# Probability-times-values matmuls issued for two key steps at a time, from one ring of four probability slots

## The chip, the cores and the metric

The kernel runs on one core of a Trainium2 chip. The metric is the device time of one execution in microseconds (us). Five engines matter: TensorE (PE, matmuls, with its weight loads shown apart as PEld), VectorE (DVE), ScalarE (ACT), GpSimd (POOL), and the DMA queue of SyncE (SP).

## What is computed

One transformer layer: a layer norm, then a latent attention and a mixture of experts side by side, both added to the input. The change lies in the attention (2 batches, 1024 tokens, 16 heads), whose core in the reference is:

```python
q_latent = x @ wq_down                       # 192 wide
kv_latent = x @ wkv_down                     # 64 wide
...
q_r = apply_rope(q_r, cos, sin)
k_r = apply_rope(k_r, cos, sin)
q = jnp.concatenate([q_c, q_r], axis=-1)
k = jnp.concatenate([k_c, k_r], axis=-1)
scores = jnp.einsum('bthd,bshd->bhts', q, k) * scale
scores = jnp.where(causal[None, None], scores, jnp.finfo(scores.dtype).min)
probs = jax.nn.softmax(scores, axis=-1)
out = jnp.einsum('bhts,bshd->bthd', probs, v).reshape(b, t, H * D)
return out @ wo
```

The kernel multiplies the probabilities with the 64 wide latent instead of `v`; `wv_up` and `wo` are folded into one matrix per head.

## The kernel before

The program has three parts: `prepare` (layer norm, latents), `attend` (attention, from about 50 to 875 us of the profile) and `mix` (the experts). Only `attend` is changed.

**Stages and steps.** `attend` runs 16 stages, s = 0 to 15: 8 pairs of heads times 2 batches (b = 0 and 1). A stage has 12 steps k. Steps 0 to 3 handle query chunk c = 0 (512 queries) against key tiles j = 0 to 3 (128 keys each), steps 4 to 11 chunk c = 1 against key tiles j = 0 to 7. Steps 0 to 3 and 8 to 11 are diagonal: their widths are 512, 384, 256 and 128 queries. In each step e = 0 and e = 1 are the two heads. Tensors are held transposed, keys on the partitions, queries along the free axis.

**What one step does.** PE computes `scores` (k, e) into one of three PSUM banks `ps_s` (lines 592 to 601). ACT takes the exponential into a probability buffer in SBUF (`exponent`, line 734). PE multiplies it with the latent: `values` (line 613) adds into the bank `ps_o`, head 0 in rows 0 to 63 and head 1 in rows 64 to 127, so that its matmuls are 64 columns wide in the array, where scores, projections and pieces are 128 wide. The text calls the pair of matmuls of step k v(k). Being float32, each of the two shows as two passes in the trace, four records in all. DVE (head 0) and POOL (head 1) add the probabilities up for the softmax's denominator (`add_probs`, lines 908 and 1060).

**Where probabilities stand.** Those of j = 0 go to `first`, one buffer per chunk and head, which is also the running sum. Those of all other steps go round a ring of three slots.

**The denominator.** PE sums the running sum over the keys with a matrix of ones (`row_sums`, line 634, also 64 wide): `Lp` for chunk 1 of the stage before, in step 2, and `L0` for chunk 0, in step 4. DVE then takes the reciprocal `rec` (line 913) and the product `on` (line 917), ACT and POOL split `on` into `ohi` and `olo` (lines 782, 1064), and PE projects them out (`Yp0`, `Yp1`, `Y0`, `Y1`, lines 644 to 646).

**Work for the next stage.** In steps 0 to 3 PE projects queries and keys of the next stage (`QR0`, `KR0`, `QR1`, `KR1`, `QL0`, `QL1`, line 550), which DVE, POOL and ACT rotate and split. From step 5 to step 11 PE computes 24 pieces p0 to p23 of the next stage's raw scores (line 566, line 569 on the diagonal), from which DVE takes row maxima (line 897). All these side products share two banks `ps_x`, and the pieces share two banks `ps_m`: p(n) waits for the maximum of p(n-2), and each side product for the reader of the one two places before.

**Order.** Every engine runs its own list in order. PE's is written by hand in `body`: `scores(k, 0)`, piece slot 0, side work 0, `scores(k, 1)`, slot 1, `values(k - 1)`, slot 2, side work 1, slot 3. The tables are

```python
PIECE_AT = dict(zip([(5, 3)] + [(k, n) for k in (6, 7, 8, 9, 10) for n in range(4)] + [(11, n) for n in range(3)],
SIDE = {(0, 0): ["QR0"], (0, 1): ["KR0"], (1, 0): ["QR1"], (1, 1): ["KR1"], (2, 0): ["Lp"], (2, 1): ["QL0"], (3, 1): ["QL1"],
        (4, 1): ["L0"], (6, 0): ["Yp0"], (6, 1): ["Yp1"], (7, 0): ["B"], (7, 1): ["WA"], (10, 0): ["Y0"], (10, 1): ["Y1"]}
```

so p0 is in step 5, p1 to p4 in step 6, p5 to p8 in step 7, p9 to p12 in step 8, p13 to p16 in step 9, p17 to p20 in step 10 and p21 to p23 in step 11. `B` and `WA` are weight folds of stages with b = 0 only. The last stage has no pieces and no projections.

Of the kernel before, what the change touches and what calls it, by code (L numbers as in the profile page):

```python
# [21 lines left out]
F32 = mybir.dt.float32  # L22
# [330 lines left out]
RING = 3  # L353


def ring_of(k):

    r = k - 1 if k < TPC else k - 2
    steps = [s for s in range(STEPS) if s not in (0, TPC)]
    if r >= RING:  # L360
        return r % RING, steps[r - RING]
    last = max(q for q in range(len(steps)) if q % RING == r % RING)
    return r % RING, steps[last] - STEPS
# [18 lines left out]
SIDE = {(0, 0): ["QR0"], (0, 1): ["KR0"], (1, 0): ["QR1"], (1, 1): ["KR1"], (2, 0): ["Lp"], (2, 1): ["QL0"], (3, 1): ["QL1"],  # L382
# [16 lines left out]
def attend(nc, d, keep):  # L399
    ctx = ExitStack()  # L400
    with ctx:
# [11 lines left out]
        t1, first, ring, shift, oe, rec, on, ohi, olo = tensors(nc, ctx, [  # L413
            ("t1", [P, 4, CH], F32), ("first", [P, 2, 2, CH], F32), ("ring", [P, RING, 2, CH], F32),
# [34 lines left out]
        def probs(k, e):  # L449
            c, j, off, _ = step_of(k)  # L450
            if j == 0:
                return first[:, c, e, off:]
            return ring[:, ring_of(k)[0], e, off:]

        def sums(s, c, j, e):


            return (sum_pool if e else sum_dve), s * 10 + (3 + j if c else j)
# [48 lines left out]
        def _(pe):  # L507
# [119 lines left out]
            def row_sums(i, b, name, s, c):  # L627

                for e in range(2):
                    pe.wait_ge(*sums(s, c, 7 if c else 3, e))  # L630

                def products(out):
                    for e in range(2):
                        mm = nc.tensor.matmul(out[64 * e:64 * e + 64, :], ones[:, 0:64], first[:, c, e, :], start=True, stop=True)  # L634
                    return mm
                side(i, b, name, products)
# [12 lines left out]
            def body(i):  # L649
                for b in range(B):  # L650
# [3 lines left out]
                    for k in range(STEPS):  # L654
# [45 lines left out]
            s = 2 * PAIRS - 1  # L700
            values(s, 1, STEPS - 1, alone=True)
# [5 lines left out]
            for e in range(2):  # L707
                mm = nc.tensor.matmul(ps_x[n % 2][64 * e:64 * e + 64, :], ones[:, 0:64], first[:, 1, e, :], start=True, stop=True)
# [9 lines left out]
        def _(act):  # L718
            def exponent(s, k, e):
# [3 lines left out]
                if j:  # L723

                    _, before = ring_of(k)
                    ge(act, pv_done, s * U + 2 * before + e + 1)
                    if before >= 0:
                        cb, jb, _, _ = step_of(before)
                        sb = s
                    else:  # L730
                        cb, jb, _, _ = step_of(before + STEPS)
                        sb = s - 1
                    ge(act, *sums(sb, cb, jb, e))
                nc.scalar.activation(probs(k, e), ps_s[(2 * k + e) % 3][:, off:], ACT.Exp, scale=SCALE).then_inc(exp_done, 1)  # L734

            def first_free(i, b, c):

                if c == 0:
                    if b == 1:
                        act.wait_ge(misc_ready, misc(i, 0, "L0")[0] + 1)  # L740
                    elif not is_first(i):
                        act.wait_ge(misc_ready, misc(i, 0, "QR0")[0] - 2)
                elif b == 1 or not is_first(i):
                    act.wait_ge(misc_ready, misc(i, b, "Lp")[0] + 1)
# [98 lines left out]
        def _(dve):  # L843
# [55 lines left out]
            def add_probs(s, k):  # L899
# [38 lines left out]
            def body(i):  # L938
                for b in range(B):
                    s = i * 2 + b  # L940
                    earlier = b == 1 or not is_first(i)
                    for k in range(STEPS):
# [25 lines left out]
                        if k % TPC or k > TPC:  # L968
                            add_probs(s, k)
# [53 lines left out]
        def _(pool):  # L1023
# [27 lines left out]
            def add_probs(s, k):  # L1051
# [3 lines left out]
                if j == 1:  # L1055

                    pool.wait_ge(pv_done, s * U + 2 * (k - 1) + 2)
                else:
                    pool.wait_ge(*sums(s, c, j - 1, 1))
                nc.gpsimd.tensor_tensor(first[:, c, 1, off:], first[:, c, 1, off:], probs(k, 1), ALU.add).then_inc(sum_pool, 1)  # L1060
# [5 lines left out]
            def body(i):  # L1066
                for b in range(B):
# [5 lines left out]
                    for k in range(1, TPC):  # L1073
                        add_probs(s, k)
# [4 lines left out]
                    for k in range(TPC + 1, STEPS):  # L1079
                        add_probs(s, k)  # L1080
# [350 lines left out]
```

## Time and profile before

| quantity | value |
| --- | --- |
| median of 3 runs | 1288.75 us (1288.48 to 1288.90) |
| profiled execution, span of the trace | 1286.1 us |
| PE busy | 1223.4 us (95%) |
| DVE busy | 905.4 us (70%) |
| POOL busy | 674.5 us (52%) |
| ACT busy | 589.7 us (46%) |

The span is the time from the first to the last instruction of one profiled execution; it is 2.65 us under the median of the runs. Matmuls overlap in the array and their ends are modelled, so the time that a matmul costs is read from its start to the start of the next one, not from its duration. A time in square brackets behind a row of a timeline is how long the engine sat idle before it, and whom it waited for.

### The profile page before, as it was taken

How to read it: one execution, taken by the hardware profiler on the slowest of the kernel's cores; microseconds unless marked ns; L12 is line 12 of the kernel's file. 1: busy time of each engine (PE TensorE's matmuls, PEld its weight loads, DVE VectorE, ACT ScalarE, POOL GpSimd, SP SyncE). 2: the span in 40 equal slices, each digit the busy share in tenths (PEclk: the TensorE clock that was granted, in tenths of full speed). 3: DMA queues.
4: the chain of work that ended last, by engine and by line, in shares of the span. 5: the costliest groups of instructions: out<-in, count | busy, mean ns of one | idle time of the engine just before them, and what ended most of it. 6: DMA issues, size and time to landing. Idle time of an engine off the chain costs nothing. (4 is left out here: it accounts for less than half of the span.)

```text
span 1286.1 us, 20218 instructions
## 1 busy us (share of the span) xinstructions
PE 1223.4 (95%) x5904; PEld 806.2 (63%) x5952; DVE 905.4 (70%) x1410; ACT 589.7 (46%) x1192; POOL 674.5 (52%) x546
## 2 busy tenths in 40 slices
PE   5898899999999999999999999998999999999997
PEld 3555455555555555555555555546788887888886
DVE  6679878879888888888888798764544445444444
ACT  3453535545545445455355365453433333333332
POOL 1176766677677667676676676652233332323332
PEclk9999999999999999999999999998999999999999
DMA  5001001001000000000100001015633333433332
GB/s 200 33 1 33 1 1 33 1 1 32 0 0 15 16 0 13 18 0 0 32 0 0 15 0 58 1 26 147 180 114 114 114 114 100 134 114 114 114 114 90
DMA packets 26442, 67.33 MB, mean 52 GB/s; under 512 B 3044, under 2 KB 9700, under 8 KB 26408
## 3 DMA queue, kind: packets, MB, share of 16 engines
q1 hardware_dynamic: 26264, 66.84, 17.2%
q8 instruction: 17, 0.28, 0.1%
q14 instruction: 17, 0.14, 0.0%
q10 hardware_dynamic: 144, 0.07, 0.0%
HBM read 62.42 MB, written 4.47 MB: 52 GB/s over the span
## 5 line engine op out<-in xcount | busy, mean ns | idle before, releaser
L734 ACT ACTIVATE ring<-ps_s 128x512 f32<-128x512 f32 (+3 forms) x320 | 146.5, 468 | 309.3 <-PE ps_s L601 308.4
L1333 POOL TENSOR_TENSOR hl<-hf,hh 128x512 fp32r<-128x512 f32 x96 | 123.4, 1286 | 288.9 <-ACT hh L1270 288.9
L897 DVE TENSOR_REDUCE nm<-ps_m 128x1 f32<-128x512 f32 (+3 forms) x370 | 196.4, 549 | 46.0 <-PE ps_m L569 39.1
L1060 POOL TENSOR_TENSOR first<-first,ring 128x512 f32<-128x512 f32 (+3 forms) x160 | 161.2, 1007 | 89.6 <-ACT ring L734 57.1
L908 DVE TENSOR_TENSOR first<-first,ring 128x512 f32<-128x512 f32 (+3 forms) x160 | 140.6, 879 | 10.1 <-ACT ring L734 5.1
L1029 POOL TENSOR_TENSOR xtf<-xtf,sinv 128x512 f32<-128x512 f32 x62 | 79.6, 1284 | 119.1 <-DVE xtf L851 119.1
L1302 DVE TENSOR_TENSOR gs<-gs,routing 128x512 f32<-128x512 f32 x64 | 44.3, 692 | 137.8 <-ACT gs L1266 137.8
L613 PE MATMUL ps_o<-ring,kvn 128*64 128x512 f32 (+3 forms) x640 | 132.4, 493 | 0.0
L1270 ACT ACTIVATE hh<-hf 128x512 fp32r<-128x512 f32 x96 | 60.7, 633 | 121.1 <-DVE hf L1307 121.1
L1266 ACT ACTIVATE gs<-ps_g 128x512 f32<-128x512 f32 x96 | 57.4, 598 | 121.3 <-PE ps_g L1225 121.3
L913 DVE RECIPROCAL rec<-ps_x 128x512 f32<-128x512 f32 x32 | 107.3, 3352 | 4.8 <-PE ps_x L634 4.0
L596 PE MATMUL ps_s<-shift,ones 128*128 128x512 bf16 (+3 forms) x336 | 109.7, 327 | 0.0
L1047 POOL TENSOR_TENSOR qlo<-t,qhi 64x512 fp32r<-64x512 f32 x64 | 94.9, 1483 | 8.6 <-POOL first L1060 2.6
L596 PEld LDWEIGHTS ps_s<-shift,ones 128*128 128x128 bf16 x384 | 37.2, 97 | 89.9 <-issue 52.0
L599 PE MATMUL ps_s<-qhi,khi 128*128 128x512 f32 (+1 forms) x192 | 87.6, 456 | 0.0
L599 PE MATMUL ps_s<-qhi,keys 128*128 128x512 f32 (+1 forms) x192 | 87.2, 454 | 0.0
L850 DVE TENSOR_TENSOR t<-ps_x,cosv 128x512 f32<-128x512 f32 x64 | 44.2, 691 | 58.6 <-PE ps_x L550 58.4
L1064 POOL TENSOR_TENSOR olo<-on,ohi 128x512 fp32r<-128x512 f32 x31 | 42.3, 1365 | 81.4 <-ACT ohi L782 81.4
L1031 POOL TENSOR_TENSOR t<-t,xtf 128x512 f32<-128x512 f32 x62 | 82.3, 1327 | 4.9
L566 PE MATMUL ps_m<-khi,qhi 128*128 128x512 f32 (+1 forms) x192 | 73.1, 390 | 8.8 <-DVE nm L897 8.6
L566 PE MATMUL ps_m<-keys,qhi 128*128 128x512 f32 (+3 forms) x178 | 68.1, 400 | 5.6 <-DVE nm L897 5.6
L1307 DVE TENSOR_TENSOR hf<-gs,ps_u 128x512 f32<-128x512 f32 x96 | 66.1, 688 | 9.9 <-PE ps_u L1225 0.6
(241 smaller groups left out, 3097.1 us busy)
## 6 DMA issues: line engine op xcount, KB each, us to landing
routing<-wT_scratch SPq DMA_DIRECT2D x34, 256.0 KB, 3.7
raw_a<-in_e SPq DMA_DIRECT2D x17, 384.0 KB, 3.0
cosv<-in_e SPq DMA_DIRECT2D x17, 384.0 KB, 3.0
sinv<-wT_scratch SPq DMA_DIRECT2D x17, 384.0 KB, 3.6
raw<-in_e SPq DMA_DIRECT2D x17, 384.0 KB, 3.0
routing<-wT_scratch SPq DMA_DIRECT2D x16, 384.0 KB, 3.3
raw_a<-in_a SPq DMA_DIRECT2D x8, 512.0 KB, 3.3
raw_b<-in_b SPq DMA_DIRECT2D x8, 480.0 KB, 3.9
```

The source lines that it names most:

```text
L566: mm = nc.tensor.matmul(out[:, 0:keys], qhi[b][e][:, t * P:(t + 1) * P], khi[b][e][:, k0:k0 + keys], start=True, stop=not diagonal)
L596: nc.tensor.matmul(out[:, off:], ones16[:, :], shift[:, c, e, off:], start=True, stop=False)
L599: nc.tensor.matmul(out[:, off:], khi[b][e][:, kk], qhi[b][e][:, q], start=False, stop=False)
L613: nc.tensor.matmul(ps_o[64 * e:64 * e + 64, off:], kvn[:, b * 8 + j, :], probs(k, e), start=j == 0, stop=last).then_inc(pv_done, 1)
L734: nc.scalar.activation(probs(k, e), ps_s[(2 * k + e) % 3][:, off:], ACT.Exp, scale=SCALE).then_inc(exp_done, 1)
L897: nc.vector.tensor_reduce(out=to, in_=bank[:, 0:keys], axis=AXX, op=ALU.max, negate=True).then_inc(piece_max, 1)
L908: nc.vector.tensor_tensor(first[:, c, 0, off:], first[:, c, 0, off:], probs(k, 0), ALU.add).then_inc(sum_dve, 1)
L913: nc.vector.reciprocal(rec[:, :], ps_x[x][:, :]).then_inc(rec_done, 1)
L1031: nc.gpsimd.tensor_tensor(t1[:, g, :], t1[:, g, :], sh[:, g, :], ALU.add).then_inc(rope_sum, 1)
L1047: nc.gpsimd.tensor_tensor(lo[to_b][e][rows, cs], t1[rows, g, :], hi[to_b][e][rows, cs].bitcast(F32), ALU.subtract).then_inc(rope_lo, 1)
L1060: nc.gpsimd.tensor_tensor(first[:, c, 1, off:], first[:, c, 1, off:], probs(k, 1), ALU.add).then_inc(sum_pool, 1)
L1333: nc.gpsimd.tensor_tensor(hl[:, c, :], hf[:, c, :], hh[:, c, :].bitcast(F32), ALU.subtract).then_inc(h_lo, 1)
```

## The change

- `values` runs in even steps only, for two key steps at once: v(k-2) and v(k-1) in step k, and v(10) and v(11) of the stage before in step 0.
- The ring has four slots and takes all steps; `ring_of` and `first` are gone. A separate `total_p` holds the running sum: step j = 1 writes it from two ring slots, later steps add one slot. In chunk 0 the slot of j = 1 is only 384 wide, so the first 128 columns are copied apart, one more instruction on DVE and on POOL per stage.
- ACT's waits before an exponential name the slot's readers of four steps before. The wait for the row sums' buffer moves from ACT to DVE and POOL (`total_free`).
- `Lp` moves from step 2's first side slot to its second, right behind the values.

```diff
-RING = 3
-
-
-def ring_of(k):
...
+RING = 4
+assert STEPS % RING == 0
...
-SIDE = {(0, 0): ["QR0"], (0, 1): ["KR0"], (1, 0): ["QR1"], (1, 1): ["KR1"], (2, 0): ["Lp"], (2, 1): ["QL0"], (3, 1): ["QL1"],
+SIDE = {(0, 0): ["QR0"], (0, 1): ["KR0"], (1, 0): ["QR1"], (1, 1): ["KR1"], (2, 1): ["Lp", "QL0"], (3, 1): ["QL1"],
...
         def probs(k, e):
-            c, j, off, _ = step_of(k)
-            if j == 0:
-                return first[:, c, e, off:]
-            return ring[:, ring_of(k)[0], e, off:]
+            return ring[:, k % RING, e, step_of(k)[2]:]
...
-                    if e or alone:
+                    if alone or (e and k % 2):
                         pe.wait_ge(exp_done, s * U + 2 * k + e + 1)
...
-                        if k:
+                        if k and k % 2 == 0:
+                            values(s, b, k - 2)
                             values(s, b, k - 1)
-                        elif earlier:
+                        elif k == 0 and earlier:
+                            values(s - 1, 1 - b, STEPS - 2)
                             values(s - 1, 1 - b, STEPS - 1)
...
+                held = (k - RING) % STEPS
+                sb = s if k >= RING else s - 1
+                cb, jb, _, _ = step_of(held)
+                ge(act, pv_done, sb * U + 2 * held + e + 1)
+                ge(act, *sums(sb, cb, max(jb, 1), e))
                 nc.scalar.activation(probs(k, e), ps_s[(2 * k + e) % 3][:, off:], ACT.Exp, scale=SCALE).then_inc(exp_done, 1)
...
-            def add_probs(s, k):
+            def add_probs(i, b, s, k):
 
                 c, j, off, _ = step_of(k)
                 dve.wait_ge(exp_done, s * U + 2 * k + 1)
-                if j == 1:
-
-                    dve.wait_ge(pv_done, s * U + 2 * (k - 1) + 1)
+                if j > 1:
+                    dve.wait_ge(*sums(s, c, j - 1, 0))
                 else:
-                    dve.wait_ge(*sums(s, c, j - 1, 0))
-                nc.vector.tensor_tensor(first[:, c, 0, off:], first[:, c, 0, off:], probs(k, 0), ALU.add).then_inc(sum_dve, 1)
+                    total_free(dve, i, b, c)
+                so_far = total_p[:, c, 0, off:] if j > 1 else probs(k - 1, 0)[:, off:]
+                nc.vector.tensor_tensor(total_p[:, c, 0, off:], so_far, probs(k, 0), ALU.add).then_inc(sum_dve, 1)
+                if k == 1:
+                    nc.vector.tensor_copy(total_p[:, 0, 0, 0:P], probs(0, 0)[:, 0:P]).then_inc(sum_dve, 1)
```

POOL's `add_probs` is changed in the same way.

PE's list from the second piece of step 8 to the last piece of step 9. `ps_m` rows are pieces, `ps_o` rows are values. Before, p14 is followed by v(8), then p15 and p16:

```order
L566 MATMUL ps_m<-keys,qhi 128x512
L613 MATMUL ps_o<-ring,kvn 64x512 x2
L51 REGISTER_ALU
L566 MATMUL ps_m<-keys,qhi 128x256
L569 MATMUL ps_m<-ident,mask 128x128
L51 REGISTER_ALU
L566 MATMUL ps_m<-keys,qhi 128x512
```

Now p14, p15 and p16 stand in a row:

```order
L564 MATMUL ps_m<-khi,qhi 128x512
L51 REGISTER_ALU
L564 MATMUL ps_m<-khi,qhi 128x256
L567 MATMUL ps_m<-ident,mask 128x128
L51 REGISTER_ALU
L564 MATMUL ps_m<-khi,qhi 128x512
```

The values have left step 9; v(8) now stands in step 10 ahead of v(9), between p18 and p19.

PE's list in step 2, from the end of `scores(2, 0)` to the start of `QL0`. Before, `Lp` (line 634) stands between the scores of the two heads and v(1) behind them:

```order
L601 MATMUL ps_s<-qhi,keys 128x256
L634 MATMUL ps_x<-first,ones 64x512 x2
L596 MATMUL ps_s<-shift,ones 128x256
L598 MATMUL ps_s<-mask,ident 128x128
L599 MATMUL ps_s<-qhi,keys 128x256
L600 MATMUL ps_s<-qlo,keys 128x256
L601 MATMUL ps_s<-qhi,keys 128x256
L613 MATMUL ps_o<-ring,kvn 64x384 x2
L550 MATMUL ps_x<-q1hi,lhi 128x512
```

Now both scores come first, then v(0), v(1) and `Lp` in a row:

```order
L599 MATMUL ps_s<-qhi,khi 128x256
L51 REGISTER_ALU
L611 MATMUL ps_o<-ring,kvn 64x512 x2
L611 MATMUL ps_o<-ring,kvn 64x384 x2
L628 REGISTER_ALU
L511 REGISTER_ALU
L632 MATMUL ps_x<-total_p,ones 64x512 x2
L511 REGISTER_ALU
L548 MATMUL ps_x<-q1hi,lhi 128x512
```

`Lp` has moved behind `scores(2, 1)`, v(0) and v(1).

## Rows read from the trace of the kernel before

**Rows 1.** Steps 2-4, then 5-11: length, busy us of PE, PEld, DVE, ACT, POOL.

```profile
439.70:452.90 13.20, 12.65 (x66) 7.03 (x66) 12.86 (x13) 9.03 (x21) 8.05 (x8) 1.00 0.00 0
452.90:479.60 26.70, 26.25 (x136) 15.23 (x138) 23.00 (x36) 12.67 (x28) 21.61 (x17) 1.00 0.00 0
```

**Rows 2.** Timeline of PE around v(4) and v(0): start, us, operation, [idle before].

```profile
452.36 0.40 PE L600 MATMUL ps_s<-qlo,khi 128*128 128x512 f32 x1
452.60 0.39 PE L601 MATMUL ps_s<-qhi,klo 128*128 128x512 f32 x1
452.92 1.08 PE L613 MATMUL ps_o<-first,kvn 128*64 128x512 f32 x4
453.93 0.33 PE L566 MATMUL ps_m<-keys,qhi 128*128 128x128 f32 x1
...
439.09 0.50 PE L550 MATMUL ps_x<-kv,rhi 128*128 128x512 f32 x1
439.42 0.40 PE L550 MATMUL ps_x<-kv,rlo 128*128 128x512 f32 x1
```

**Rows 3.** Timeline of PE: v(11) alone; v(3) followed by L0, last stage.

```profile
434.27 0.44 PE L613 MATMUL ps_o<-ring,kvn 128*64 128x128 f32 x4
434.64 0.50 PE L550 MATMUL ps_x<-kv,rhi 128*128 128x512 f32 x1
...
840.48 0.44 PE L613 MATMUL ps_o<-ring,kvn 128*64 128x128 f32 x4
840.75 1.05 PE L634 MATMUL ps_x<-first,ones 128*64 128x512 f32 x4
```

**Rows 4.** Timeline of PE, steps 2 to 4: Lp, scores(2, 1), v(1), QL0, QL1, L0.

```profile
440.34 1.08 PE L634 MATMUL ps_x<-first,ones 128*64 128x512 f32 x4
441.35 0.28 PE L596 MATMUL ps_s<-shift,ones 128*128 128x256 bf16 x1
...
442.03 0.87 PE L613 MATMUL ps_o<-ring,kvn 128*64 128x384 f32 x4
442.83 0.50 PE L550 MATMUL ps_x<-q1hi,lhi 128*128 128x512 f32 x1
...
445.93 0.50 PE L550 MATMUL ps_x<-q1hi,lhi 128*128 128x512 f32 x1 [0.17 <-DVE rec L913]
...
449.96 1.08 PE L634 MATMUL ps_x<-first,ones 128*64 128x512 f32 x4 [0.39 <-DVE first L908]
```

**Rows 5.** Timeline of DVE, steps 2 to 5 of the same stage.

```profile
441.11 1.50 DVE L908 TENSOR_TENSOR first<-first,ring 128x384 f32<-128x384 f32 x1
442.53 3.35 DVE L913 RECIPROCAL rec<-ps_x 128x512 f32<-128x512 f32 x1
...
449.54 0.29 DVE L908 TENSOR_TENSOR first<-first,ring 128x128 f32<-128x128 f32 x1
...
454.95 1.66 DVE L917 TENSOR_TENSOR on<-oe,rec 128x512 f32<-128x512 f32 x1 [0.29 <-POOL olo L1064]
```

**Rows 6.** Timelines of POOL and PE, steps 5 and 6: olo, Yp0, v(5), p3.

```profile
453.54 1.27 POOL L1064 TENSOR_TENSOR olo<-on,ohi 128x512 fp32r<-128x512 f32 x1 [5.64 <-ACT ohi L782]
...
455.24 0.47 PE L644 MATMUL ps_x<-ohi,bhi 128*128 128x512 f32 x1
...
457.31 1.08 PE L613 MATMUL ps_o<-ring,kvn 128*64 128x512 f32 x4
458.70 0.49 PE L566 MATMUL ps_m<-keys,qhi 128*128 128x512 f32 x1 [0.32 <-DVE nm L897]
```

**Rows 7.** Timeline of DVE: p10, p11 and p12, add(8) in step 8; p19 in step 10.

```profile
466.66 0.69 DVE L897 TENSOR_REDUCE nm<-ps_m 128x1 f32<-128x512 f32 x1 [0.36 <-PE ps_m L566]
467.99 0.97 DVE L897 TENSOR_REDUCE nm<-ps_m 128x1 f32<-128x128 f32 x2 [0.65 <-PE ps_m L569]
468.88 1.65 DVE L908 TENSOR_TENSOR first<-first,ring 128x512 f32<-128x512 f32 x1
...
475.70 0.56 DVE L897 TENSOR_REDUCE nm<-ps_m 128x1 f32<-128x384 f32 x1 [0.54 <-PE ps_m L569]
```

More of the change, by code:

```diff
@@ L350, in step_of @@
     return c, j, max(0, j * P - c * CH), j * P >= c * CH
-RING = 3
-def ring_of(k):
[L358 to L363, printed above, removed]
+RING = 4
+assert STEPS % RING == 0
 def pieces():
@@ L412, in attend @@
         sh = keep["xtf"][:, :, :].rearrange("p k (g c) -> p (k g) c", c=CH)
-        t1, first, ring, shift, oe, rec, on, ohi, olo = tensors(nc, ctx, [
-            ("t1", [P, 4, CH], F32), ("first", [P, 2, 2, CH], F32), ("ring", [P, RING, 2, CH], F32),
+        t1, total_p, ring, shift, oe, rec, on, ohi, olo = tensors(nc, ctx, [
+            ("t1", [P, 4, CH], F32), ("total_p", [P, 2, 2, CH], F32), ("ring", [P, RING, 2, CH], F32),
             ("shift", [P, 2, 2, CH], BF16), ("oe", [P, CH], F32), ("rec", [P, CH], F32), ("on", [P, CH], F32),
@@ L449, in probs, with total_free @@
         def probs(k, e):
-            c, j, off, _ = step_of(k)
-            if j == 0:
-                return first[:, c, e, off:]
-            return ring[:, ring_of(k)[0], e, off:]
+            return ring[:, k % RING, e, step_of(k)[2]:]
         def sums(s, c, j, e):
-            return (sum_pool if e else sum_dve), s * 10 + (3 + j if c else j)
+            return (sum_pool if e else sum_dve), s * 11 + (4 + j if c else 1 + j)
+        def total_free(engine, i, b, c):
+            if c == 0:
+                if b == 1:
+                    engine.wait_ge(misc_ready, misc(i, 0, "L0")[0] + 1)
+                elif not is_first(i):
+                    engine.wait_ge(misc_ready, misc(i, 0, "QR0")[0] - 2)
+            elif b == 1 or not is_first(i):
+                engine.wait_ge(misc_ready, misc(i, b, "Lp")[0] + 1)
         def consumed(i, b, name):
@@ L633, in products @@
                     for e in range(2):
-                        mm = nc.tensor.matmul(out[64 * e:64 * e + 64, :], ones[:, 0:64], first[:, c, e, :], start=True, stop=True)
+                        mm = nc.tensor.matmul(out[64 * e:64 * e + 64, :], ones[:, 0:64], total_p[:, c, e, :], start=True, stop=True)
                     return mm
@@ L700, in _ @@
             s = 2 * PAIRS - 1
+            values(s, 1, STEPS - 2, alone=True)
             values(s, 1, STEPS - 1, alone=True)
@@ L707, in _ @@
             for e in range(2):
-                mm = nc.tensor.matmul(ps_x[n % 2][64 * e:64 * e + 64, :], ones[:, 0:64], first[:, 1, e, :], start=True, stop=True)
+                mm = nc.tensor.matmul(ps_x[n % 2][64 * e:64 * e + 64, :], ones[:, 0:64], total_p[:, 1, e, :], start=True, stop=True)
             mm.then_inc(misc_ready, 1)
@@ L722, in exponent @@
                 act.wait_ge(scores_ready, u + 1)
[L723 to L733, printed above, removed]
-                nc.scalar.activation(probs(k, e), ps_s[(2 * k + e) % 3][:, off:], ACT.Exp, scale=SCALE).then_inc(exp_done, 1)
[L736 to L744, printed above, removed]
+                held = (k - RING) % STEPS
[3 more added lines that the diff above has]
+                ge(act, *sums(sb, cb, max(jb, 1), e))
+                nc.scalar.activation(probs(k, e), ps_s[(2 * k + e) % 3][:, off:], ACT.Exp, scale=SCALE).then_inc(exp_done, 1)
             def latent_hi(i, b, c, to_b):
@@ L1049, in rope_low, with add_probs @@
                 pool.wait_ge(rope_lo, s * 8 + 2 * g + 2)
-            def add_probs(s, k):
+            def add_probs(i, b, s, k):
                 c, j, off, _ = step_of(k)
                 pool.wait_ge(exp_done, s * U + 2 * k + 2)
-                if j == 1:
-                    pool.wait_ge(pv_done, s * U + 2 * (k - 1) + 2)
-                else:
-                    pool.wait_ge(*sums(s, c, j - 1, 1))
-                nc.gpsimd.tensor_tensor(first[:, c, 1, off:], first[:, c, 1, off:], probs(k, 1), ALU.add).then_inc(sum_pool, 1)
+                if j > 1:
+                    pool.wait_ge(*sums(s, c, j - 1, 1))
+                else:
+                    total_free(pool, i, b, c)
+                so_far = total_p[:, c, 1, off:] if j > 1 else probs(k - 1, 1)[:, off:]
+                nc.gpsimd.tensor_tensor(total_p[:, c, 1, off:], so_far, probs(k, 1), ALU.add).then_inc(sum_pool, 1)
+                if k == 1:
+                    nc.gpsimd.tensor_copy(total_p[:, 0, 1, 0:P], probs(0, 1)[:, 0:P]).then_inc(sum_pool, 1)
             def out_low(s, c):
@@ L1079, in body @@
                     for k in range(TPC + 1, STEPS):
-                        add_probs(s, k)
+                        add_probs(i, b, s, k)
                         if k == 7:
```

6 lines of the change are left out of this document (2 added, 4 removed).

## The prediction, made before the result was known

> **What bounds the kernel now.** I read the page's busy shares first: PE 95%, DVE 70%. That suggests a kernel bound by PE, and the change takes work from PE. But DVE's 70% is an average over a part that hardly uses it (the experts) and the attention, so the second view is the busy time by stretch of one attention stage [rows 1]. In steps 2 to 4 DVE is busy 12.86 of 13.20 us; in steps 5 to 11 it is busy 23.00 of 26.70 us, while PE is busy 12.65 and 26.25. Both engines are nearly full, each in the other's cover. The third view, the timelines, shows where each waits for the other. PE waits for DVE at QL1 (0.17 us, for the reciprocal of Lp) and at L0 (0.39 us, for the last sum of chunk 0) [rows 4], and at p3 (0.32 us, for a maximum) [rows 6]. DVE waits for PE's pieces: 0.36 us for p10, 0.65 us for p11, 0.54 us for p19 [rows 7]. With two banks for pieces, neither can be more than two pieces from the other.
>
> **What one merge saves on PE.** An ordinary 512-column matmul follows its predecessor after 0.24 us (452.36 to 452.60), the first values matmul after 0.32 us, and the matmul behind a group also takes longer, 0.33 us (439.09 to 439.42) [rows 2]. So entering costs 0.08 and the successor 0.09 to 0.10 us. What a group itself loses is seen where two groups of this kind already follow each other: in the last stage L0 starts 0.27 us after v(3), while v(11), of the same 128 columns, holds PE for 0.37 us when it stands alone (434.27 to 434.64) [rows 3]. That is 0.10 us for leaving. A further 0.05 us is the first pass of a second group that needs no filling (L0 spans 1.05 us there, 1.08 elsewhere; I take the upper figure). The sum is about 0.33 us for a merge. Width: v(4) alone takes 1.01 us for 512 columns [rows 2], v(11) 0.37 us for 128 [rows 3], so 128 columns are 0.21 us and the bodies are 0.86, 0.64, 0.43 and 0.21 us for 512, 384, 256 and 128 columns.
>
> A stage has twelve values groups before and six after, so six merges, and Lp, which stood alone, joins v(1). Its successor is a bf16 matmul that pays nothing (the row of scores(2, 1) begins at once [rows 4]), so that merge gives 0.23 us. PE's work falls by 6 x 0.33 + 0.23 = 2.2 us per stage, 35 us over 16 stages.
>
> **What moves.** v(10) goes from step 11 into step 0 of the next stage, and the values of steps 1, 3, 5, 7 and 9 go one step later. So even steps get two values at once, up to 1.85 us in which PE makes no piece, and odd steps get none. I walk one stage from its first score and write how much later (+) or earlier (-) each point comes.
>
> *Steps 0 to 2.* v(10) comes in with its body less what is kept: +0.43 in step 0. v(0) leaves step 1: 0.86 body and 0.33 switch, -1.2. So PE arrives at step 2 0.8 us early. But Lp is now behind scores(2, 1) (0.68 us, 441.35 to 442.03 [rows 4]), v(0) and v(1). Its start is 440.34 - 0.8 - 0.08 + 0.68 + 0.05 + 0.86 + 0.64 = 441.7, its end 1.05 us later, 442.75. The reciprocal started at 442.53, held back only by DVE's own add(1), which began at 441.11 [rows 5]. It now waits for PE: **+0.2 us**. The new 128-column copy on DVE lies in this wait. The trace has no such copy; the nearest row is the 128-column sum with 0.29 us [rows 5], below is nothing. POOL's copy ends long before POOL's 5.64 us of idling ahead of olo [rows 6], so it costs nothing; if that cover were gone its price would be a POOL instruction, under the 1.27 us of a 512-column one.
>
> *Steps 2 to 4.* From the reciprocal on, DVE's chain sets the pace: reciprocal 3.35 us, on, sums and low parts without a gap, until add(3) ends at 449.83 and L0 starts at 449.96 [rows 4, 5]. QL1 needs the reciprocal's end, now 442.75 + 3.35 = 446.1 instead of 445.9. PE gets there much earlier than before: QL0 starts at about 442.65, and v(2) is no longer in between, so it arrives at about 444.8 and idles 1.3 us (0.17 before). L0 is bound by add(3) as before. So all that PE has saved by here, and the outgoing v(4) too, is idle time, and scores(5, 0) starts at **+0.2 us**.
>
> *Steps 5 to 7.* v(4) is gone from step 5 (-1.2), but Yp0 needs olo, which POOL ends at 454.81 [rows 6] and which hangs on the same chain: now 455.0, where PE would arrive at 454.25. And p2 needs the bank of p0, whose maximum follows on (454.95 to 456.61, moved by 0.2). So v(4) and v(5) start at +0.15 and last 0.86 us longer; the 0.32 us wait at p3 [rows 6] and the bound of p2 absorb some, p3 comes at +0.6. Step 7 has no values and gives 1.2 back, of which DVE, with four maxima and a sum in that step, lets through about half: scores(8, 0) at 0.
>
> *Steps 8 to 11.* v(6) and v(7) delay p11 and p12 by 0.84 us. DVE, which finished p10 at 467.35 and waited 0.65 us, now waits 1.5 us. Then come p11 to p16 with no values between them: DVE needs 0.97 us for p11 and p12 and up to 1.65 us for add(8) [rows 7], and two banks let PE no further ahead, so PE idles at p15 and p16 and gets to step 10 between 0.1 us (add(8) taking half its time) and 0.8 us late. v(8) and v(9) add 0.86 us ahead of p19: DVE waits about 1.4 us there instead of 0.54. Step 11 has lost v(10), but there DVE is the slower one (four maxima of 512 columns, 0.69 us each [rows 7], the addition of Y1 and two sums), so nothing comes back. The next stage starts **0.9 to 1.6 us later**. Cross-check: DVE's 23.0 us of work in steps 5 to 11 is the same, so this stretch grows by as much as DVE's 3.7 us of idling; the walk has it growing by 0.7 to 1.4 us.
>
> I take 1.2 us, the middle, since the stages differ in how DVE's sums meet POOL. It holds for 15 stages; the last one has no pieces and no projections, and I give it PE's whole saving, -2. ACT's new waits name readers of four steps before, which in the walk have always ended. Sum: 1286.1 + 15 x 1.2 - 2 = 1302.1 us of span, and with the 2.65 us between span and median **1304.8 us**.
>
> **Rivals.**
>
> *PE's saving comes through (faster).* If DVE's idle time stretches and shrinks freely, the bursts do no harm: then only the bound of steps 2 to 4 stays (+0.2), and steps 5 to 11 get their three merges (1.0) and the outgoing v(10) (0.43 + 0.33) for nothing: -1.6 per stage, 15 x 1.6 + 2 = 26 us, 1262.8 us. For it: PE's gaps are small, 0.4 us in the 26.7 us. Against it: DVE has no more than 3.7 us of idling there, in pieces of 0.2 to 1 us which the bursts enlarge. At the extreme Lp binds nothing either and all 35 us come, 1254 us.
>
> In the Trainium skill's page on TensorEngine Tiling, section Key Properties, a change of the tiling mode drains the engine while a change of tile does not; that is the same 0.33 us as a mechanism, and by that rule alone the result would be this rival's. Here the trace agrees on the price (0.27 against 0.37 us) but not that PE's time is what counts.
>
> *The two effects cancel (same).* If add(8) and add(9) meet POOL less, and step 7 gives back its whole 1.2 us, a stage ends at about +0.1: 15 x 0.1 - 2 is nothing that can be told.
>
> *Merged groups don't stream.* If two values of different steps do need the full switch between them, PE gains nothing and only loses in the bursts: another 0.33 us at p3, p11 and p19 each, of which the waits hide half, +0.5 per stage, 1312 us. Against it stands the pair v(3), L0 [rows 3].
>
> **How the numbers follow.** Slower as walked 0.57, not streaming 0.04, cancelling 0.09, faster 0.30. About 0.2%, 2.6 us, is what a measurement of this kernel can tell from no change. Slower by more: 0.61; within: 0.09; faster: 0.30. The forecast's own range is 15 x 0.9 - 2 to 15 x 1.6 - 2, 1300 to 1311 us. The range for 8 in 10 must reach the faster rival's middle, 1262, and at the top 1311; 0.1 is left out on either side.
>
> **What would show it.** Right: in the profile after, v(0), v(1) and Lp follow without gaps; PE idles over 1 us at QL1 behind the reciprocal; waits of the pieces for maxima and of maxima for pieces both grow; DVE's busy time is the same. The stage is about 1.2 us longer. Wrong: PE idle at QL1 but none at p15, p16, p21 to p23, or DVE without a wait at p11 and p19; then the stage gets shorter and the faster rival holds. It also falls if a values pair holds PE for much less than 1.8 us.

## The result, and the profile after

The changed kernel takes 1315.43 us (median of 4 runs, 1315.05 to 1319.31), the kernel before 1288.83 us beside it: a ratio of 1.0207, 95% interval 1.0193 to 1.0222. It is slower, as forecast, but by 26.6 us where 16 were forecast, and lies outside the range given.

The span of the profiled execution is 1317.5 us, 31.4 us more than before. The profiled execution was the slowest of the four (1319.31 us), which is most of why this exceeds 26.6 us. Of the 31.4 us 23.0 lie in the twelve stages 2 to 13 (1.92 us each), 5.65 in stages 0 and 1, 1.5 in stage 14, 0.4 in stage 15, 1.1 between its last score and the attention's last matmul, and 1.3 before the attention's first score; the experts behind it are 1.5 us shorter. In stages 2 to 14 the granted clock is 1.00 in both profiles.

The page's first lines of the changed kernel: PE's busy time has fallen by 10.5 us, DVE's has risen by 6.0. (The trace before has 48 records of PE fewer, 5904, all bf16 matmuls of the scores, so PE's fall is somewhat larger than that.)

```profile
span 1317.5 us, 20308 instructions
## 1 busy us (share of the span) xinstructions
PE 1212.9 (92%) x5952; PEld 821.5 (62%) x5952; DVE 911.4 (69%) x1426; ACT 587.9 (45%) x1192; POOL 683.8 (52%) x562
```

The two stretches of [rows 1], in the same stage (7) of the changed kernel: steps 2 to 4, then 5 to 11; length, then busy us of PE, PEld, DVE, ACT, POOL.

```profile
455.00:469.30 14.30, 13.02 (x71) 7.72 (x71) 12.96 (x15) 10.09 (x25) 9.25 (x9) 1.00 0.00 0
469.30:497.20 27.90, 26.20 (x134) 15.30 (x133) 23.46 (x36) 12.65 (x28) 21.95 (x17) 1.00 0.00 0
```

The first stretch holds v(0) in addition. The second has lost v(10), with v(4) moved inside it from step 5 to step 6, and yet it is 1.2 us longer (27.90 against 26.70). DVE is busy 0.46 us longer in it and idle 0.74 us longer.

Timeline of PE in steps 2 to 4, which answers to [rows 4], and of DVE, which answers to [rows 5]:

```profile
456.27 1.72 PE L611 MATMUL ps_o<-ring,kvn 128*64 128x512 f32 x8
457.82 1.03 PE L632 MATMUL ps_x<-total_p,ones 128*64 128x512 f32 x4
458.78 0.50 PE L548 MATMUL ps_x<-q1hi,lhi 128*128 128x512 f32 x1
...
462.31 0.50 PE L548 MATMUL ps_x<-q1hi,lhi 128*128 128x512 f32 x1 [1.18 <-DVE rec L899]
```

```profile
456.45 1.07 DVE L892 TENSOR_TENSOR total_p<-ring 128x384 f32<-128x384 f32 x1
457.44 0.31 DVE L894 COPY total_p<-ring 128x128 f32<-128x128 f32 x1
458.90 3.36 DVE L899 RECIPROCAL rec<-ps_x 128x512 f32<-128x512 f32 x1 [1.15 <-PE ps_x L632]
```

v(0), v(1) and Lp follow without gaps and hold PE for 2.51 us (456.27 to 458.78). The prediction's bodies (0.86, 0.64 and 0.86 us) and its 0.15 us for leaving and for the first pass give the same 2.51. The reciprocal now waits 1.15 us for PE, and PE idles 1.18 us at QL1 for the reciprocal, 0.17 before.

Timeline of DVE in steps 8 to 10, which answers to [rows 7], and of PE around the two bursts and step 9:

```profile
485.12 0.98 DVE L881 TENSOR_REDUCE nm<-ps_m 128x1 f32<-128x128 f32 x2 [1.50 <-PE ps_m L567]
486.02 1.22 DVE L892 TENSOR_TENSOR total_p<-total_p,ring 128x512 f32<-128x512 f32 x1
...
493.28 0.56 DVE L881 TENSOR_REDUCE nm<-ps_m 128x1 f32<-128x384 f32 x1 [1.41 <-PE ps_m L567]
```

```profile
482.82 1.94 PE L611 MATMUL ps_o<-ring,kvn 128*64 128x512 f32 x8
484.69 0.33 PE L564 MATMUL ps_m<-keys,qhi 128*128 128x128 f32 x1
...
487.62 0.39 PE L564 MATMUL ps_m<-keys,qhi 128*128 128x256 f32 x1 [0.22 <-DVE nm L881]
...
496.39 0.49 PE L564 MATMUL ps_m<-keys,qhi 128*128 128x512 f32 x1 [0.44 <-DVE nm L881]
```

Behind each burst of two values (the first takes 1.87 us, from 482.82 to 484.69) DVE sits idle for a piece: 1.50 us at p11, 0.65 before; 1.41 us at p19, 0.54 before. And PE waits for DVE where the odd steps have lost their values, at p15 (487.62), and in step 11 at p23 (496.39).

Two lines from the waits of the whole run, of the changed kernel and then of the kernel before (total us, times, longest): DVE waits for diagonal pieces 14 us longer, PE for maxima 18 us longer.

```profile
DVE nm L881 <- PE ps_m L567: 53.3, 55, 3.1
PE ps_m L564 <- DVE nm L881: 32.6, 52, 3.2
```

```profile
DVE nm L897 <- PE ps_m L569: 39.1, 72, 1.4
PE ps_m L566 <- DVE nm L897: 14.3, 26, 2.9
```

### The profile page after: what moved, and what is told of

Its sections match the earlier page's. It is cut to its first block and busy times, and to the rows that moved or that the text cites. A ratio compares the mean times of both kernels' runs of the same rounds, so it can differ in the third digit from the quotient of the medians.

```text
span 1317.5 us, 20308 instructions
## 1 busy us (share of the span) xinstructions
PE 1212.9 (92%) x5952; PEld 821.5 (62%) x5952; DVE 911.4 (69%) x1426; ACT 587.9 (45%) x1192; POOL 683.8 (52%) x562
## 5 line engine op out<-in xcount | busy, mean ns | idle before, releaser
L730 ACT ACTIVATE ring<-ps_s 128x512 f32<-128x512 f32 (+3 forms) x384 | 181.5, 489 | 398.4 <-PE ps_s L599 397.1
L1046 POOL TENSOR_TENSOR total_p<-total_p,ring 128x512 f32<-128x512 f32 (+3 forms) x128 | 124.6, 973 | 100.3 <-ACT ring L730 79.2
L611 PE MATMUL ps_o<-ring,kvn 128*64 128x512 f32 (+3 forms) x768 | 147.1, 504 | 0.0
L594 PE MATMUL ps_s<-shift,ones 128*128 128x512 bf16 (+3 forms) x384 | 128.7, 335 | 3.1 <-DVE nm L881 2.5
L892 DVE TENSOR_TENSOR total_p<-total_p,ring 128x512 f32<-128x512 f32 (+3 forms) x128 | 101.2, 791 | 5.5 <-ACT ring L730 4.7
L611 PEld LDWEIGHTS ps_o<-ring,kvn 128*64 128x64 f32 x768 | 47.0, 137 | 65.9 <-issue 58.0
```

Source lines behind the costliest of these rows:

```text
L594: nc.tensor.matmul(out[:, off:], ones16[:, :], shift[:, c, e, off:], start=True, stop=False)
L892: nc.vector.tensor_tensor(total_p[:, c, 0, off:], so_far, probs(k, 0), ALU.add).then_inc(sum_dve, 1)
L1046: nc.gpsimd.tensor_tensor(total_p[:, c, 1, off:], so_far, probs(k, 1), ALU.add).then_inc(sum_pool, 1)
```

## The experiments

All of them but the ones that start from the kernel before are built from the changed kernel. Ratios are to the kernel before, run beside them on the same chip. A shift of a point is the mean over stages 2 to 13 of its distance from the last matmul of the stage's first score, less the same of the kernel before. Runs on different chips are compared by their medians; the medians of the kernel before on these chips lie between 1288.8 and 1290.4 us, so such a difference is good to about 1.5 us. Of a line of the tables only the entries that differ are shown.

Six use one table for what is issued where, with the values of the stage before as negative numbers:

```diff
+VALUES = {0: [-2, -1], 2: [0, 1], 4: [2, 3], 5: [4], 6: [5], 7: [6], 8: [7], 9: [8], 10: [9]}
...
-                        if k and k % 2 == 0:
-                            values(s, b, k - 2)
-                            values(s, b, k - 1)
-                        elif k == 0 and earlier:
-                            values(s - 1, 1 - b, STEPS - 2)
-                            values(s - 1, 1 - b, STEPS - 1)
+                        for v in VALUES.get(k, ()):
+                            if v >= 0:
+                                values(s, b, v)
+                            elif earlier:
+                                values(s - 1, 1 - b, STEPS + v)
```

The wait inside `values` and the values behind the last stage follow the table as well.

### The ring alone: ring4_single

```diff
+VALUES = {0: [-1], 1: [0], 2: [1], 3: [2], 4: [3], 5: [4], 6: [5], 7: [6], 8: [7], 9: [8], 10: [9], 11: [10]}
...
-(2, 1): ["Lp", "QL0"]
+(2, 0): ["Lp"], (2, 1): ["QL0"]
```

> The changed kernel with its four-slot ring, total_p and the extra copy, but with the values matmuls issued one key step at a time as before, and Lp back in its old place. If the grouping is what costs (my theory), this is close to the kernel before: the copy adds 0.2 us to DVE's chain in each stage, so +3 us, 1292 us. If the ring, the separate sum or the moved waits cost, it stands near the changed kernel's 1315 us.

Measured: 1291.24 us, ratio 1.0019 (1.0007 to 1.0032). Ring, separate sum, copy and moved waits together cost 2 us over the kernel, 0.26 us in each of stages 2 to 13. At scores(5, 0) the shift is already +0.38. The reciprocal starts 0.25 us later, since add(1) and the copy lie in DVE's chain ahead of it when nothing else makes it wait, and `on` behind it takes 1.80 instead of 1.67 us.

### Only the late values in pairs: late_pairs

```diff
+VALUES = {0: [-1], 1: [0], 2: [1], 3: [2], 4: [3], 6: [4, 5], 8: [6, 7], 10: [8, 9], 11: [10]}
...
-(2, 1): ["Lp", "QL0"]
+(2, 0): ["Lp"], (2, 1): ["QL0"]
```

> As ring4_single, but the values of steps 4 to 9 go in pairs (in steps 6, 8 and 10). My theory, the bursts next to the two piece banks: from scores(5, 0) to the stage's end the changed kernel lost 1.5 us per stage, so this one takes 15 x 1.5 = 22 us more than ring4_single, about 1313 us. If PE's saved switches counted it would be 1 us per stage less than ring4_single, about 1277 us. If the loss sits in steps 0 to 4, it equals ring4_single.

Measured: 1316.25 us, ratio 1.0212 (1.0189 to 1.0235), 25 us more than ring4_single. Up to scores(5, 0) the shift is +0.39, the same as ring4_single; p3 comes at +0.72, p11 at +1.28, p19 at +1.88, the stage's end at +1.88. Three merges that save PE a switch each cost 1.6 us per stage.

### Only the early values in pairs: early_pairs

The table is the one shown first; Lp stays behind v(1).

> The changed kernel with pairs only in steps 0, 2 and 4 (v(10) and v(11), v(0) and v(1) with Lp behind them, v(2) and v(3)); the values of steps 4 to 9 one at a time. My theory: steps 0 to 4 cost 0.4 us per stage, and v(10) leaves step 11, where DVE is the bound, for little: 1288.8 + 6 = 1295 us, within 3 us. If the late pairs are harmless it stays near 1315 us.

Measured: 1291.03 us, ratio 1.0014 (1.0002 to 1.0026), 4 us better than expected. The shift at scores(5, 0) is +0.38 and +0.25 at the end. So the changed kernel without the pairs of steps 6, 8 and 10 loses nothing against its ring. This number hides two effects that cancel, as early_pairs_lp20 shows below: with Lp back in its place the same pairs gain about 15 us, and Lp behind v(1) costs about 15.

### Lp back in its place: after_lp20

```diff
-(2, 1): ["Lp", "QL0"]
+(2, 0): ["Lp"], (2, 1): ["QL0"]
```

> The changed kernel with only Lp put back between the scores of step 2. My theory: the reciprocal then waits for DVE's own add and not for PE, and starts 0.7 to 0.9 us earlier; all that follows to scores(5, 0) hangs on it. So 0.9 us per stage less than the changed kernel, 13 us, 1302 us. If the pairs alone set the pace, it is the changed kernel's time plus one switch per stage, 1315 to 1319 us.

Measured: 1297.60 us, ratio 1.0073 (1.0054 to 1.0092), 18 us less than the changed kernel where 13 were expected. scores(5, 0) moves from +0.38 to -0.14, by only 0.5 us; the stage's end from +1.92 to +0.54, by 1.4. The earlier chain is worth more behind it than at its end: Yp0, p2 and p3, which wait for it, come 1.2 us earlier (p2 +0.22 to -0.94, p3 +0.77 to -0.39). Besides the 0.5 us this is the second `on` of the stage, which takes 1.20 us on average instead of 1.66. That the burst of step 6 does less harm for it is my reading of these shifts; no run isolates it.

### Both together: early_pairs_lp20

```diff
+VALUES = {0: [-2, -1], 2: [0, 1], 4: [2, 3], 5: [4], 6: [5], 7: [6], 8: [7], 9: [8], 10: [9]}
...
-(2, 1): ["Lp", "QL0"]
+(2, 0): ["Lp"], (2, 1): ["QL0"]
```

> Pairs only in steps 0, 2 and 4, single values in steps 5 to 10, and Lp back between the scores of step 2. If the two parts add up as the runs so far suggest (putting Lp back gave the changed kernel 18 us, going single late gave it 24 us), it is about 1274 us, faster than both kernels. My theory of the parts alone gives 0.9 us per stage for Lp against early_pairs, 1291 - 13 = 1278 us. The rival, that with single values late DVE is the bound of steps 5 to 11 whatever comes before, gives 1288 to 1291 us.

Measured: 1276.65 us, ratio 0.9898 (0.9882 to 0.9915): faster than both kernels. What the early pairs give is there, as long as Lp isn't put behind them.

### DVE's load cut: before_light and after_light

```diff
-                nc.vector.tensor_reduce(out=to, in_=bank[:, 0:keys], axis=AXX, op=ALU.max, negate=True).then_inc(piece_max, 1)
+                nc.vector.tensor_reduce(out=to, in_=bank[:, 0:64], axis=AXX, op=ALU.max, negate=True).then_inc(piece_max, 1)
...
-                nc.vector.reciprocal(rec[:, :], ps_x[x][:, :]).then_inc(rec_done, 1)
+                w = CH if isinstance(s, int) and s < 2 else 128
+                nc.vector.reciprocal(rec[:, 0:w], ps_x[x][:, 0:w]).then_inc(rec_done, 1)
```

> The kernel before with DVE's load cut: every row maximum reads 64 columns only, and the reciprocal is taken of 128 columns from the third stage on (both change the result). It is the base for after_light. DVE loses about 24 x 0.4 and 2 x 2.5 us of its 42 us per stage, so only PE is left as a bound: 1270 to 1280 us.

> The changed kernel with the same cut of DVE's load. If DVE next to PE is why the saved switches don't pay (my theory), they pay here: 2.2 us per stage less than before_light, up to 35 us, at least 20 us less, 1240 to 1255 us. If the grouped values cost on PE itself (no streaming, a longer chain through ACT), it stays slower than before_light by 10 us or more.

Measured: 1261.78 us (ratio 0.9782, 0.9765 to 0.9799) and 1254.32 us (0.9721, 0.9704 to 0.9738). The base gained more than expected. With DVE light the change turns from a loss of 26.6 us into a gain of 7.5 us. That shows that DVE next to PE is what turned its sign. The gain is a third of what was expected at the least. In stages 2 to 13 it is 0.9 us per stage; stages 0 and 1, in which the reciprocal is whole, are 5.4 us longer than before_light's, at a granted clock of 0.97 and 0.94 against 1.00 in both. Stages 2 to 13, of before_light and then of after_light: length, then busy us of PE, PEld, DVE, ACT, POOL.

```profile
170.78:755.46 584.68, 577.73 (x3026) 335.99 (x3025) 360.87 (x745) 304.91 (x672) 412.95 (x336) 1.00 0.03 10
176.42:750.48 574.06, 562.07 (x3026) 345.06 (x3025) 357.02 (x757) 302.07 (x672) 419.16 (x349) 1.00 0.03 10
```

PE's busy time falls by 1.3 us per stage, where 2.2 were forecast, and its idle time grows by 0.4. One wait of PE has come in, for olo at Yp0, 9.0 us in all; before_light has none there. The reciprocal's wait for the row sums has doubled, with Lp in its new place. The first row and the last are of after_light, the one between is of before_light; total us, times, longest:

```profile
PE ps_x L642 <- POOL olo L1053: 9.0, 12, 0.8
DVE rec L914 <- PE ps_x L634: 12.1, 16, 2.6
DVE rec L900 <- PE ps_x L632: 27.9, 29, 4.1
```

DVE's waits for diagonal pieces are about the same in both (92.4 and 87.7 us). Why PE's busy time falls by only 1.3 us of the 2.2 was not tested.

### POOL's load cut: after_port and before_port

In the changed kernel half of the stages 2 to 13 are longer than the others (2.1 to 2.3 us over before, against 1.5 to 1.7). They part at add(6), which takes 1.8 us in the long ones and 0.68 in the short ones, and 0.8 us in each of these stages of the kernel before. Timelines of POOL and DVE of the changed kernel, in stage 7 and in stage 9:

```profile
477.55 3.21 POOL L1033 TENSOR_TENSOR keys<-t,keys 64x512 fp32r<-64x512 f32 x2 [0.22 <-POOL total_p L1046]
...
477.56 0.68 DVE L892 TENSOR_TENSOR total_p<-total_p,ring 128x512 f32<-128x512 f32 x1
...
580.27 2.96 POOL L1033 TENSOR_TENSOR keys<-t,keys 64x512 fp32r<-64x512 f32 x2 [0.22 <-POOL total_p L1046]
...
580.30 1.81 DVE L892 TENSOR_TENSOR total_p<-total_p,ring 128x512 f32<-128x512 f32 x1
```

Where DVE's sum starts within 0.01 us of POOL's subtraction it takes 0.68 us, where it starts 0.03 us behind it takes 1.81. In its page SBUF — State Buffer, section "SBUF: two separate sides", the Trainium skill says that a DVE instruction with two SBUF inputs and a GpSimd instruction that reads SBUF take the shared pair of ports whole: the one that starts first gets it, and the other is blocked. The second pair of rows agrees, with 1.1 us for DVE as the loser. In the first pair the starts are too close to tell who came first; DVE is not held up, and POOL's two subtractions take 3.21 instead of 2.96 us.

```diff
+                    w = slice(c * CH, c * CH + (CH if isinstance(s, int) and s < 2 else 16))
-                    nc.gpsimd.tensor_tensor(lo[to_b][e][rows, cs], t1[rows, g, :], hi[to_b][e][rows, cs].bitcast(F32),
+                    nc.gpsimd.tensor_tensor(lo[to_b][e][rows, w], t1[rows, g, 0:w.stop - w.start], hi[to_b][e][rows, w].bitcast(F32),
                                             ALU.subtract).then_inc(rope_lo, 1)
```

> The changed kernel with POOL's subtractions for the low parts of the rotated queries and keys cut from 512 to 16 columns from the third stage on (this changes the result); DVE, PE and ACT do what they did. Theory: in about half of the stages DVE's add(6) starts just after such an instruction of POOL and takes 1.8 instead of 0.7 us, which makes the stage 0.9 us longer. Without them these stages are as short as the others, and the adds of steps 8 to 11 shorten too: 1315 - 7 to 1315 - 20, 1295 to 1308 us. If POOL has no part in it, 1315 us.

> The kernel before with the same cut of POOL's low-part subtractions as in after_port (this changes the result). after_port took 5 us less than the changed kernel. If the port meetings are something that the change brought in by shifting DVE's add(6), this one gains less than that, 0 to 3 us: 1287 to 1290 us. If POOL's load costs the kernel before as much, it gains 5 us too, 1284 us.

Measured: after_port 1310.13 us, ratio 1.0150 (1.0131 to 1.0170); before_port 1282.88 us, ratio 0.9953 (0.9936 to 0.9971). The alternation is gone, stages 2 to 13 of after_port are 1.2 to 1.4 us longer than those of the kernel before, and scores(8, 0) comes at +0.02 instead of +0.45. But the kernel before gains as much from the same cut. Against the kernel before on its own chip after_port costs 19.8 us and the changed kernel 26.6, a gain of 6.8 us, and before_port gains 6.7. With POOL light the change costs 26.5 us, with POOL as it is 26.6. So the meetings with POOL explain why the stages alternate, and where in a stage the loss falls, but not that it is larger than forecast. The expectation that this was the change's own cost is refuted.

### The burst taken apart: late_split

```diff
+VALUES = {0: [-1], 1: [0], 2: [1], 3: [2], 4: [3], 6: [4, 5], 8: [6, 7], 10: [8, 9], 11: [10]}
...
                         maxima(0)
+                        for v in VALUES.get(k, ())[:-1]:
+                            values(s, b, v, alone=True)
                         side_work(0)
...
                         maxima(1)
+                        for v in VALUES.get(k, ())[-1:]:
...
```

> late_pairs with the two values of an even step apart: the first behind the first head's scores and piece, the second behind the second head's. PE's work is as in ring4_single (no switch saved), the values of odd steps are still missing, but the gap between two pieces is 1.0 us at most, as before, and no more 1.85 us. If the unbroken gap starves DVE (my theory), most of the 25 us between late_pairs (1316 us) and ring4_single (1291 us) is gone: 1293 to 1300 us. If it is the odd steps without values, where PE runs ahead into the two banks, it stays at 1310 us or more.

Measured: 1309.66 us, ratio 1.0154 (1.0138 to 1.0171): 7 us of the 25 are gone, 18 stay. By its own terms this speaks against the unbroken gap as the main cause and for the unevenness between steps. At s(10, 0) the shift is still small (+0.29, late_pairs +1.02), so steps 5 to 9 are in fact nearly repaired; the loss comes in step 10 (p19 at +1.44). Timeline of late_split there, PE and then DVE:

```profile
483.72 1.08 PE L614 MATMUL ps_o<-ring,kvn 128*64 128x512 f32 x4
484.73 0.50 PE L645 MATMUL ps_x<-ohi,bhi 128*128 128x512 f32 x1
...
486.12 0.40 PE L567 MATMUL ps_m<-keys,qhi 128*128 128x512 f32 x1
```

```profile
485.83 0.69 DVE L912 TENSOR_TENSOR yacc<-yacc,ps_x 128x512 f32<-128x512 f32 x1 [1.11 <-PE ps_x L647]
486.55 0.69 DVE L884 TENSOR_REDUCE nm<-ps_m 128x1 f32<-128x512 f32 x1
...
487.79 0.56 DVE L884 TENSOR_REDUCE nm<-ps_m 128x1 f32<-128x384 f32 x1 [0.54 <-PE ps_m L570]
```

v(8) now stands ahead of Y0, whose sum DVE must do before it may go on to p18: it idles 1.11 us for it. So this run mixes two things: the split repairs steps 5 to 9, and puts another product that DVE waits for behind a values group. How the 18 us divide between that and the values missing from step 9 is not settled.

### Without the pair in step 0: pairs_2_4

```diff
+VALUES = {0: [-1], 2: [0, 1], 4: [2, 3], 5: [4], 6: [5], 7: [6], 8: [7], 9: [8], 10: [9], 11: [10]}
...
-(2, 1): ["Lp", "QL0"]
+(2, 0): ["Lp"], (2, 1): ["QL0"]
```

> early_pairs_lp20 (1277 us) without its pair in step 0: v(10) goes back to step 11. My theory has DVE as the bound of step 11, so v(10) there costs nothing and one switch more costs nothing either: 1277 us, within 2 us. If v(10)'s move out of step 11 made the gain, 1285 to 1290 us.

Measured: 1268.56 us, ratio 0.9841 (0.9823 to 0.9860). Neither expectation holds: it is 8 us faster than early_pairs_lp20. v(10) back in step 11 costs nothing there, as the theory has it (the shift stays -1.24 from p3 to the end), but out of step 0 it is not free: Lp comes 0.43 us earlier. The chain behind it, DVE's timeline of pairs_2_4 in the same stage:

```profile
433.31 1.02 DVE L895 COPY total_p<-ring 128x128 f32<-128x128 f32 x1
434.25 3.35 DVE L900 RECIPROCAL rec<-ps_x 128x512 f32<-128x512 f32 x1
437.63 0.69 DVE L904 TENSOR_TENSOR on<-oe,rec 128x512 f32<-128x512 f32 x1
438.24 1.51 DVE L893 TENSOR_TENSOR total_p<-total_p,ring 128x256 f32<-128x256 f32 x1
...
442.94 3.36 DVE L900 RECIPROCAL rec<-ps_x 128x512 f32<-128x512 f32 x1
```

and of early_pairs_lp20:

```profile
437.54 3.35 DVE L901 RECIPROCAL rec<-ps_x 128x512 f32<-128x512 f32 x1
440.92 1.70 DVE L905 TENSOR_TENSOR on<-oe,rec 128x512 f32<-128x512 f32 x1
442.54 1.50 DVE L894 TENSOR_TENSOR total_p<-total_p,ring 128x256 f32<-128x256 f32 x1
```

The reciprocal itself starts only 0.23 us earlier in its stage (9.56 against 9.79 us behind the last matmul of the first score; before, 10.78). But then `on` takes 0.69 instead of 1.70 us. POOL's rows beside it, of pairs_2_4 and then of early_pairs_lp20:

```profile
437.72 1.75 POOL L1016 TENSOR_TENSOR xtf<-xtf,sinv 128x512 f32<-128x512 f32 x1
...
440.79 1.29 POOL L1017 TENSOR_TENSOR xtf<-xtf,sinv 128x512 f32<-128x512 f32 x1
```

In pairs_2_4 `on` starts 0.09 us before POOL's product and POOL's takes 1.75 us; in early_pairs_lp20 it starts 0.13 us behind and DVE's takes 1.70. One meeting won instead of lost, 1.0 us, makes up most of the difference at scores(5, 0) (-1.32 against -0.15). By the end of the stage half of that difference is gone (-1.24 against -0.67), which is the 8 us. No run separates the meeting from v(10)'s move.

### Lp behind the values there: pairs_2_4_lp21

```diff
-(2, 0): ["Lp"], (2, 1): ["QL0"]
+(2, 1): ["Lp", "QL0"]
```

> pairs_2_4 (1269 us) with Lp moved behind v(0) and v(1) in step 2, as the change has it. My theory: the reciprocal waits for PE again and L0 follows it. Without v(10) in step 0 PE is 0.4 us earlier than in the changed kernel, so scores(5, 0) comes 0.0 us after that of the kernel before instead of 1.3 us ahead of it: 15 x 1.3 = 20 us more, 1289 us, within 4 us. If only the order of v(10) mattered, it stays within 3 us of 1269 us; if Lp's saved switch counts, 1265 us.

Measured: 1286.81 us, ratio 0.9975 (0.9963 to 0.9986), 18 us more than pairs_2_4. Lp comes 2.1 us later, scores(5, 0) 1.2 us. That is as expected, and the same 18 us that putting Lp back gave the changed kernel. The reciprocal starts 1.1 us later and carries the shift alone; `on` is short here too (0.74 to 0.87 us).

### The sum

| step | time | difference |
| --- | --- | --- |
| kernel before | 1288.8 to 1290.4 us | |
| + ring of four, separate sum (ring4_single) | 1291.2 | +2 |
| + pairs in steps 2 and 4 (pairs_2_4) | 1268.6 | -23 |
| + v(10) paired in step 0 (early_pairs_lp20) | 1276.7 | +8 |
| + pairs in steps 6, 8 and 10 (after_lp20) | 1297.6 | +21 |
| + Lp behind v(1) (the changed kernel) | 1315.4 | +18 |

The rows are medians from different chips, good to about 1.5 us, and the edits are not independent: Lp behind v(1) costs about 15 us in early_pairs, and 18 in the changed kernel and in pairs_2_4_lp21. Taken in this order the changed kernel is one good edit and three bad ones, on a ring that costs 2 us. pairs_2_4 is 1.6% faster than the kernel before and 47 us faster than the changed one.

## Why the prediction was right or wrong

**What bounds the kernel.** Right, and the light runs show it: with DVE's load cut the sign turns. The forecast of slower rested on this alone.

**The price of a switch and the streaming of merged groups.** Right. v(0), v(1) and Lp hold PE for 2.51 us, which is what the prediction's terms add up to; v(6) and v(7) for 1.87, forecast 1.85. The rival that groups don't stream is refuted. The whole of PE's saving is less sure: of the 2.2 us per stage the busy time of the light runs shows 1.3.

**The walk, point by point** (mean of stages 2 to 13):

| point | forecast | measured |
| --- | --- | --- |
| scores(5, 0) | +0.2 | +0.38 |
| p3 | +0.6 | +0.77 |
| scores(8, 0) | 0 | +0.45 |
| p11 | +0.84 | +1.36 |
| scores(10, 0) | +0.1 to +0.8 | +1.10 |
| next stage | +0.9 to +1.6, taken 1.2 | +1.92 |

The waits came where the walk had them: DVE's idle times of 1.5 us at p11 and 1.4 us at p19 were forecast as 1.5 and 1.4. What failed is the size of terms of the walk, which ends at +1.92 instead of +1.2.

The step that failed most is the one that has step 7 "give 1.2 back, of which DVE", with its four maxima and a sum, "lets through about half: scores(8, 0) at 0". From p3 to scores(8, 0) only 0.32 us came back on average, and scores(8, 0) stands at +0.45. I took DVE's instructions at the lengths they had in the trace of before, though each sum's length depends on how it meets POOL, and every meeting is shifted when a point moves. In half of the stages add(6) took 1.8 us in this way, where before it took 0.8. The two port runs correct the conclusion that this is a cost of its own. Measured from before_port, after_port loses 0.79 us from scores(5, 0) to p3, where 0.4 were forecast, and gets 0.74 back by scores(8, 0); over both together it stands 0.05 us later. With POOL as it is the two together are 0.07 us. The walk had them give 0.2 us. So what it had wrong, with either load of POOL, is that steps 5 to 7 give back more than the burst of step 6 takes. Which instruction of DVE withholds it is open.

The second term is steps 0 to 4, +0.38 for +0.2: the reciprocal started 0.29 us later on average, for 0.2, and `on` behind it took 1.75 instead of 1.67 us. The two make up 0.46 of the 0.72 us; the rest is 0.07 to 0.13 us too little for each of the three stretches from scores(8, 0) on. The sentence that counts "the outgoing v(4)" among what PE saves in steps 2 to 4 is a slip, since v(4) stood in step 5; no number hangs on it.

**The last stage and the first ones.** "I give it PE's whole saving, -2" was wrong: the last stage is 0.4 us longer to its last score, and 1.5 us to the attention's last matmul. Even with no pieces the row sums tie PE to DVE, as the timeline of PE in that stage shows:

```profile
873.28 1.08 PE L632 MATMUL ps_x<-total_p,ones 128*64 128x512 f32 x4 [1.25 <-DVE total_p L892]
```

L0 arrives earlier and waits 1.25 us for add(3), which stands behind the reciprocal. Stage 0 is 4.1 us longer in the profiled execution, more than any other. There the granted clock differs, 0.92 on average against 1.00 in the same stage before, from the busy time by stretch of the changed kernel and of the kernel before:

```profile
77.00:133.00 56.00, 49.26 (x245) 30.46 (x243) 43.16 (x111) 24.91 (x55) 33.41 (x28) 0.92 0.06 19
```

```profile
76.00:127.00 51.00, 46.78 (x242) 27.21 (x244) 42.42 (x108) 24.92 (x55) 33.01 (x27) 1.00 0.07 21
```

A mean of 0.92 is time spent at the lower of the two levels, 1.2 GHz, for part of the stage. Why it fell there was not tested. Stage 0 is also 2.8 us longer in ring4_single, whose time is only 2 us above before, with 2.4 us given back in stage 1; there the clock is 0.94 in stage 0 and 1.00 in stage 1, while the kernel before has 1.00 and 0.94. So how much of the 26.6 us belongs to the clock in the first two stages is open; in stages 2 to 14 it has no part.

**Lp's move.** The forecast had its saved switch (0.23 us) and its delay of the reciprocal, but put the delay at 0.2 us against the kernel before, and so hid that it ate up what the early pairs give. The right comparison is with Lp left in place: in after_lp20 the reciprocal starts 1.3 us earlier than in the changed kernel, and the kernel takes 18 us less. That all that PE has saved by scores(5, 0) is idle time was true, and it was Lp's move that made it so.

**The copy.** Costed at nothing behind the wait for Lp, it is indeed hidden there (457.44 to 457.75, the reciprocal at 458.90). With Lp in its old place and single values the cover is gone: in ring4_single the reciprocal starts 0.25 us later than before. The forecast's price without cover, a POOL instruction under 1.27 us, was for POOL's copy, not for this one.

**The faster rival** assumed that DVE's idling can take up the bursts. Refuted by late_pairs: 25 us more than ring4_single. A gain of that kind exists only with the late values single and Lp left in place: 14 us below the kernel before in early_pairs_lp20, 21 us in pairs_2_4.

## What to carry to other kernels

Two engines that were each 86 to 98% busy in a stretch, coupled by two buffers, behaved here as one resource: work saved on the one counts only where it doesn't stand in front of what the other waits for, and even placement of filler work was worth more than the switches it cost. Group work of the leading engine where the other is bound by its own long chain, and keep it single where they hand small pieces to and fro; and don't put the matmul that starts a long chain (here row sums ahead of a 3.4 us reciprocal) behind such a group to save a switch. When a walk through a timeline is made with durations of the old trace, ask which of them were lucky: the same sum took 0.7 or 1.8 us, depending on whether it started 0.01 or 0.03 us behind an instruction of POOL.

## What the runs showed of the hardware

A DVE sum of 512 columns took 0.68 us when it started 0.01 us behind POOL's subtraction and 1.81 us when it started 0.03 us behind it. DVE's product `on` took 0.69 us when it started 0.09 us ahead of POOL's product, which then took 1.75 us, and 1.70 us when it started 0.13 us behind, with 1.29 us for POOL's. A 128-column copy on DVE took 0.31 us, and 1.02 us in pairs_2_4, where it started 0.40 us behind a sum of POOL's and ended with it. Two values groups of 512 columns in a row hold PE for 1.87 us, alone 1.01 us each, so the second costs 0.86 us.
